# A state-space layer's depthwise convolution: from VectorE taps to diagonal matmuls, with one POOL/DVE split changed beside it

## The reference

```python
x, z = jnp.split(u @ in_w.T, 2, axis=-1)
xpad = jnp.pad(x, ((0, 0), (D_CONV - 1, 0), (0, 0)))
xc = conv_b + sum((xpad[:, k:k + L, :] * conv_w[:, k] for k in range(D_CONV)))   # D_CONV = 4
x = jax.nn.silu(xc)
xdbl = x @ xp_w.T                                  # 16 for dt, 16 for B, 16 for C
dt = jax.nn.softplus(xdbl[..., :DT_RANK] @ dt_w.T + dt_b)
dA, dBx = jnp.exp(dt[..., None] * A), (dt * x)[..., None] * Bm[:, :, None, :]
h = a * h + bx;  y = einsum('bdn,bn->bd', h, c)    # a scan over the 56 positions
y = (ys + x * Dp) * jax.nn.silu(z);  return y @ out_w.T
```

## Time and profile before

| What | us |
|---|---|
| median of three runs | 6076.04 (6052.26 to 6079.0) |
| the profiled execution | 6076.68 |
| its span, first to last instruction | 6074.9 |
| busy: DVE / POOL | 5261.9 / 5284.9 |
| busy: PE / ACT | 4575.6 / 3463.7 |
| mean granted TensorE clock | 0.871 of full speed |
| `prepare` and `attention` | until about 315 |
| `mambas`, first half: first scan at | 370.8 |
| `mambas`, second half: first scan at | 3109.2 |
| `finish` begins | 5798.6 |

### The profile page before, as it was taken

One profiled execution on the slowest core, in us unless ns is written; L12 is line 12 of the kernel. 1 busy time (PEld: TensorE's weight loads), 2 busy tenths in 40 slices (PEclk: granted clock), 3 DMA queues, 4 the chain that ended last, 5 costly groups with the idle time before them and its releaser, 6 DMA issues. The chain is left out here.

```text
span 6074.9 us, 66572 instructions
## 1 busy us (share of the span) xinstructions
PE 4575.6 (75%) x23774; PEld 3368.0 (55%) x23774; DVE 5261.9 (87%) x4001; ACT 3463.7 (57%) x5270; POOL 5284.9 (87%) x2694
## 2 busy tenths in 40 slices
PE   6957777777777777777667877777777777777689
PEld 5835555555555555555535555555555555555544
DVE  3469999999999999999969999999999999999900
ACT  0046666666666666666546666666666666666511
POOL 0059999999999999999959999999999999999900
PEclk8978888888888888888878888888888888888899
DMA  4123323232231322323123223232231323323164
GB/s 152 69 105 95 107 62 107 62 103 90 79 107 62 104 83 84 109 62 104 59 78 98 86 83 107 62 104 78 88 108 61 107 68 98 98 71 104 55 210 142
DMA packets 220096, 563.52 MB, mean 93 GB/s; under 512 B 27794, under 2 KB 94226, under 8 KB 218228
## 3 DMA queue, kind: packets, MB, share of 16 engines
q1 hardware_dynamic: 203956, 532.52, 28.0%
q10 hardware_dynamic: 15808, 26.75, 1.2%
HBM read 499.06 MB, written 60.13 MB: 92 GB/s over the span
## 5 line engine op out<-in xcount | busy, mean ns | idle before, releaser
L879 POOL TENSOR_TENSOR dbx<-dtx,b_all 128x896 f32<-128x896 f32 x1792 | 3701.3, 2091 | 0.2
L701 ACT ACTIVATE mamba_ps<-dt,w 128x448 f32<-128x448 f32 x3584 | 2136.4, 629 | 1660.5 <-DVE hc L828 1213.9
L654 PE MATMUL mamba_ps<-ident,hc 128*112 128x128 f32 x14336 | 2096.9, 300 | 968.2 <-POOL hc L886 944.1
L654 PEld LDWEIGHTS mamba_ps<-ident,hc 128*112 128x112 f32 x14336 | 1804.1, 147 | 1413.6 <-POOL hc L886 1053.6
L821 DVE TENSOR_TENSOR_SCAN mamba_ps<-mamba_ps,dbx 128x896 f32<-128x896 f32 x1120 | 2252.1, 2011 | 67.1 <-POOL dbx L879 61.7
L821 DVE TENSOR_TENSOR_SCAN hc<-mamba_ps,dbx 128x896 f32<-128x896 f32 x672 | 1353.1, 2013 | 141.3 <-ACT mamba_ps L701 141.3
L886 POOL TENSOR_TENSOR hc<-hc,c_all 128x896 f32<-128x896 f32 x672 | 1402.6, 2087 | 67.6 <-DVE hc L821 64.8
L828 DVE TENSOR_TENSOR hc<-mamba_ps,c_all 128x896 f32<-128x896 f32 x1120 | 1214.7, 1085 | 78.5 <-DVE mamba_ps L821 2.4
L582 PE MATMUL mamba_ps<-u,w 128*128 128x448 f32 x1792 | 881.4, 622 | 198.4 <-DVE x L801 142.8
L582 PEld LDWEIGHTS mamba_ps<-u,w 128*128 128x128 f32 x1792 | 365.2, 226 | 454.8 <-issue 224.8
L619 PE MATMUL mamba_ps<-w,sz 128*112 128x256 f32 x1792 | 491.2, 435 | 72.1 <-DVE sz L810 72.1
(11 more groups left out here) (98 smaller groups left out, 2597.5 us busy)
## 6 DMA issues: line engine op xcount, KB each, us to landing
b_all<-bc_scratch SPq DMA_DIRECT2D x448, 448.0 KB, 6.4
c_all<-bc_scratch SPq DMA_DIRECT2D x448, 448.0 KB, 6.1
u<-u_scratch SPq DMA_DIRECT2D x56, 448.0 KB, 8.8
y_scratch<-ytok SPq DMA_DIRECT2D x56, 448.0 KB, 3.2
src<-y_scratch SPq DMA_DIRECT2D x56, 448.0 KB, 4.6
xb<-in_x SPq DMA_DIRECT2D x4, 3136.0 KB, 12.0
u_scratch<-ub ACTq DMA_DIRECT2D x28, 448.0 KB, 8.2
src<-in_x SPq DMA_DIRECT2D x28, 448.0 KB, 6.8
```

Source lines behind the costliest of these rows:

```text
L654: ins = nc.tensor.matmul(y_ps[j % 2][:, c * 128:(c + 1) * 128], hc[g][:, e * T + c * TCH:e * T + (c + 1) * TCH], ident[:, :], start=False, ...
L701: ins = nc.scalar.activation(decay[g % 2][:, e * T:(e + 1) * T], blk(dt[t % 2], j), ACT.Exp, scale=w[:, c:c + 1])
L879: nc.gpsimd.tensor_tensor(view(dbx[g % BX_RING], 0, [[T, 2], [1, T]]), view(dtx[t % 2], j * T, [[0, 2], [1, T]]), view(b_all, 2 * g * T, [ ...
```

## The change

The convolution is made by PE. DVE makes, at the start of a half, 16 diagonal matrices of the convolution's weights (`taps`), beside the four of `skip`. ACT takes x_j as a plain copy. Four new items a tile, c0 to c3, are each four matmuls, a diagonal matrix by x_j shifted by 0 to 3 positions within each sequence, summed in a work bank; ACT takes c_j with the bias into x_j's place. `silu_x` follows c3. The DVE taps go. SCHEDULE has the new items, and y3 is made, taken and gated earlier. To make room in SBUF for `taps` the ring of dbx has 6 buffers and not 8. And POOL weighs 10 of 32 slots where it weighed 12.

```diff
 SCHEDULE = {
-    "x0": (0, 2), "x1": (2, 3), "x2": (5, 6), "x3": (7, 8), "y3": (10, None), "out0": (13, 14), "out1": (15, 16),
-    "y0": (16, None), "xp": (18, 19), "dt0": (19, 20), "dt1": (20, 21), "dt2": (21, 22), "dt3": (22, 23), "y1": (23, None),
-    "z0": (24, 25), "z1": (26, 27), "z2": (27, 28), "z3": (28, 29), "y2": (30, None),
+    "x0": (0, 1), "x1": (1, 2), "c0": (3, 5), "c1": (4, 6), "y3": (6, None), "x2": (7, 8), "x3": (9, 10), "c2": (10, 11),
+    "c3": (12, 13), "out0": (13, 14), "out1": (15, 16), "y0": (16, None), "xp": (18, 19), "dt0": (19, 20), "dt1": (20, 21),
+    "dt2": (21, 22), "dt3": (22, 23), "y1": (23, None), "z0": (24, 25), "z1": (26, 27), "z2": (27, 28), "z3": (28, 29),
+    "y2": (30, None),
 }
-FRONT = ("x0", "x1", "x2", "x3", "xp", "dt0", "dt1", "dt2", "dt3", "z0", "z1", "z2", "z3")
+FRONT = ("x0", "x1", "c0", "c1", "x2", "x3", "c2", "c3", "xp", "dt0", "dt1", "dt2", "dt3", "z0", "z1", "z2", "z3")
-MID, END = 0, 1
-TAP_AT = {
-    (2, MID): (0, 1), (2, END): (0, 2), (3, MID): (0, 3), (3, END): (1, 1), (5, MID): (1, 2), (5, END): (1, 3),
-    (7, MID): (2, 1), (7, END): (2, 2), (8, MID): (2, 3), (8, END): (3, 1), (10, MID): (3, 2), (10, END): (3, 3),
-}
-TAKE_Y_AT = {4: 3, 12: 0, 20: 1, 28: 2}
-GATE_AT = {11: 3, 16: 0, 24: 1, 31: 2}
+TAKE_Y_AT = {3: 3, 12: 0, 20: 1, 28: 2}
+GATE_AT = {7: 3, 16: 0, 24: 1, 31: 2}
-BX_RING, HC_RING = 8, 8
+BX_RING, HC_RING = 6, 8
 def by_pool(n):
-    return n % GP in (1, 4, 6)
+    return n % (2 * GP) in (1, 4, 6, 10, 14)
...
-        skip = sb("skip", DB * 128)
+        skip, taps = sb("skip", DB * 128), sb("taps", DB * DCONV * 128)
...
+                def conv(t, j):
+                    raw = Item(t, f"x{j}")
+                    pe.wait_ge(work_free[raw.slot], raw.freed())
+                    b = take(Item(t, f"c{j}"))
+                    for back in range(DCONV):
+                        k = (j * DCONV + DCONV - 1 - back) * 128
+                        ins = nc.tensor.matmul(seqs(b[:, 0:T])[:, :, back:SEQ], taps[:, k:k + 128],
+                                               seqs(blk(x[t % 2], j))[:, :, 0:SEQ - back], start=(back == 0), stop=(back == DCONV - 1))
+                    ins.then_inc(work_ready, 1)
...
-                        pe.wait_ge(skip_ready, t // TILES * DB + DB)
+                        pe.wait_ge(diag_ready, t // TILES + 1)
...
+                        nc.scalar.copy(blk(x[t % 2], j), take(it)[:, 0:T]).then_inc(work_free[it.slot], 1)
+                    elif name[0] == "c":
                         nc.scalar.activation(blk(x[t % 2], j), take(it)[:, 0:T], ACT.Identity,
-                                             scale=w[:, W_CW + j * DCONV + DCONV - 1:W_CW + (j + 1) * DCONV],
-                                             bias=w[:, W_CB + j:W_CB + j + 1]).then_inc(acc_ready, 1)
+                                             bias=w[:, W_CB + j:W_CB + j + 1]).then_inc(work_free[it.slot], 1)
...
-                nc.vector.tensor_tensor_scan(dst, h, dbx[g % BX_RING][:, :], 0.0, ALU.mult, ALU.add).then_inc(scan_done, 1)
+                nc.vector.tensor_tensor_scan(dst, h, dbx[n % BX_RING][:, :], 0.0, ALU.mult, ALU.add).then_inc(scan_done, 1)
...
+                        for k in range(DB * DCONV):
+                            ins = nc.vector.tensor_scalar_mul(taps[:, k * 128:(k + 1) * 128], ident[:, :], w[:, W_CW + k:W_CW + k + 1])
+                        ins.then_inc(diag_ready, 1)
-                        for j, back in TAP_AT.values():
-                            conv_tap(t, j, back)
```

More of the change, by code:

```diff
@@ L474, in mambas @@
         work_ready, work_free = sem("work_ready"), [sem(f"work_free{p}") for p in range(2)]
-        acc_ready, conv_chain = sem("acc_ready"), sem("conv_chain")
         silu_ready = sem("silu_ready")
@@ L481, in mambas @@
         scan_done, hc_ready, pc_ready, sums_done = sem("scan_done"), sem("hc_ready"), sem("pc_ready"), sem("sums_done")
-        skip_ready, ytr_ready = sem("skip_ready"), sem("ytr_ready")
+        diag_ready, ytr_ready = sem("diag_ready"), sem("ytr_ready")
         ones_set, restart_set = sem("ones_set"), sem("restart_set")
@@ L607, in front_item @@
                         in_proj(t, name, int(name[1]) * 128)
+                    elif name[0] == "c":
+                        conv(t, int(name[1]))
                     elif name[0] == "z":
@@ L723, in silu_x @@
                 def silu_x(t):
-                    it = Item(t, "x3")
+                    it = Item(t, "c3")
                     act.wait_ge(work_free[it.slot], it.freed())
@@ L790, in _ @@
             def _(dve):
[L791 to L805, removed]
                 def gate(t, j):
@@ L834, in _ @@
                         for j in range(DB):
-                            nc.vector.tensor_scalar_mul(skip[:, j * 128:(j + 1) * 128], ident[:, :], w[:, W_D + j:W_D + j + 1]).then_inc(skip_ready, 1)
-                        for j, back in TAP_AT.values():
-                            conv_tap(t, j, back)
+                            nc.vector.tensor_scalar_mul(skip[:, j * 128:(j + 1) * 128], ident[:, :], w[:, W_D + j:W_D + j + 1])
+                        for k in range(DB * DCONV):
+                            ins = nc.vector.tensor_scalar_mul(taps[:, k * 128:(k + 1) * 128], ident[:, :], w[:, W_CW + k:W_CW + k + 1])
+                        ins.then_inc(diag_ready, 1)
                     for n in range(SLOTS):
@@ L847, in _ @@
                                 gate(t - 1, j)
-                        if not last(t) and (n, MID) in TAP_AT:
-                            conv_tap(t + 1, *TAP_AT[n, MID])
                         if not by_pool(n):
                             weigh(SLOTS * t + n)
-                        if not last(t) and (n, END) in TAP_AT:
-                            conv_tap(t + 1, *TAP_AT[n, END])
                     if last(t):
@@ L878, in make_dbx @@
                     upto(pool, scan_done, n + 1 - BX_RING)
-                    nc.gpsimd.tensor_tensor(view(dbx[g % BX_RING], 0, [[T, 2], [1, T]]), view(dtx[t % 2], j * T, [[0, 2], [1, T]]),
+                    nc.gpsimd.tensor_tensor(view(dbx[n % BX_RING], 0, [[T, 2], [1, T]]), view(dtx[t % 2], j * T, [[0, 2], [1, T]]),
                                             view(b_all, 2 * g * T, [[T, 2], [1, T]]), ALU.mult).then_inc(dbx_ready, 1)
```

## The result

The changed kernel takes 6039.4 us (median of 20 runs, 6021.4 to 6058.9) against 6075.6 for the one before (20 runs), a ratio of 0.9949, 95% interval 0.9937 to 0.9961. It is faster by half a percent, where 2.3% were forecast; the time lies inside the range of 5865 to 6050, near its upper end. The profiled execution took 6041.8 us, its span 6040.0.

The account below looks back on a forecast made before the run. DVE with ACT's lateness was taken as the bound, POOL 1.2 us a tile behind. Saving 3.2 us in 54 periods (-173) plus 30 for fronts gave -143 from 6076.7: 5934 us, own range 5895 to 5975, stated range 5865 to 6050.

Parts of the forecast that it names:

- a tile without PE's clock: Each of 54 periods: 95.6 - 3.1 (DVE) + 1.1 (silu_z) - 1.2 (out1) = 92.4 us.
- new stall behind silu_z: Slot 3: ACT's chain takes 7.4 us, DVE without taps only 6.3, so a new stall of +1.1 a tile.
- stall behind silu_x: Slots 16 and 17: the scan was 2.23 us late; a shorter wait for out1 takes 1.2 off.
- PE's part of a tile: Convolutions on PE: 32 matmuls, 12.8 to 19.6 us a tile, costed at nothing within a tile.
- fronts: Serial stretch before each half's first scan: 28 us for 13.4, +15 a half, +30 in all (+25 to +38).
- DVE's sum: DVE's tile before: scans, weighs, taps and bare weighs 90.7 us, plus 2.6 waiting and 2.3 for gates, 95.6.
- POOL's floor: POOL's tile after the change: 44 passes, 89.8 + 0.4 = 90.2 us, below the 92.4 forecast.
- signs of being wrong: DVE waits for POOL in each tile, ACT waits for a convolution or dt, or the period is above 94.
- The 0.4 that is left of 2.6 (softplus) stays: Of DVE's 2.6 us a tile waiting for ACT, 0.4, put down to softplus, was to stay unchanged.
- The rival that said so: PE's lower clock delays dt blocks in each tile: period 96.4, 6152 us; decides above 36 of 54 periods; chance 0.11.
- the second rival: PE late in slots 10 to 15, out1's wait grows by some 0.7: 94.3 a tile, 6037 us; chance 0.19.
- out1's bound: ACT's wait for out1 at slot 16: change between 0 and -1.4, taken as -1.2; range effect 65 us up, 11 down.

Follow-up runs that it names:

- two kernels: Changed kernel with out1 taken at slot 17, y3 at slot 4 and POOL weighing 12 of 32 slots, 6020.5 us; kernel before with out1 at slot 17, 6003.1 us.
- The run that fills it: Changed kernel plus three extra matmuls, their result overwritten, on PE between x_proj's sums and dt0: 5915.1 us, ratio 0.9742.
- one number: Kernel before, taps still on DVE, with ACT taking out1 at slot 17, behind silu_x: 6003.1 us, ratio 0.9896.
- 5912: Changed kernel with z0 made by PE right behind xp at slot 18, not 24, and taken by ACT at slot 19: 5912.1 us, ratio 0.9730.
- both entries moved: Changed kernel with ACT taking out1 at slot 17, behind silu_x, and y3's sums at slot 4, behind silu_z: 5868.4 us, ratio 0.9663.
- out1 alone: Changed kernel with only ACT's take of out1 moved to slot 17, behind silu_x: 5903.4 us, ratio 0.9731.

## Why the prediction was wrong, point by point

| Step | Forecast | Measured |
|---|---|---|
| a tile without PE's clock | 92.4 us | 92.63 |
| new stall behind silu_z | +1.1 | 0.98 |
| stall behind silu_x | 1.03 | 1.32 |
| PE's part of a tile | 12.8 to 19.6, costs nothing | 12.6 busy; costs nothing by its length |
| stalls at the dt items | 0.4, as before | 0.2 in 18 periods, 2.0 to 4.0 in 36 |
| mean period | 92.4 | 94.27 and 94.75 |
| POOL | 90.2, not binding | not binding; as a bound 94.2 at 12 slots |
| fronts | +30 (25 to 38) | +7.1 and at most +13.8 |
| last tiles | 0 | +2.3 each |

**Right:** what bound the kernel, DVE's sum to two tenths of a microsecond (with 0.3 too little at slot 17 made up by 0.1 and 0.2 too much at slots 4 and 25), the stall behind silu_z, POOL's floor (two kernels sit on it, at 94.2 and 94.3), PE having room for the convolutions. The period of the undisturbed tile stands in the profile as forecast. Two of the signs of being wrong that the prediction named came about: ACT waits for dt, and the mean period is above 94.

**Wrong** is the sentence "The 0.4 that is left of 2.6 (softplus) stays". It held what the dt items cost to be unchanged, since none of their instructions were, and gave all of it to softplus; behind four dt items at the higher level it is 0.19, and the other 0.2 was the clock's already. Each of 36 periods loses 2 to 4 us there, 101 us over all: 54 x 92.63 would be 165 us less than before, and 63.5 came. The rival that said so was there, with its price (4.0 a tile; the long periods are 2.0 to 3.9 above 92.63, but for one of 5.9 at the start) and its turning point (36 periods), and it had 0.11, for two reasons that did not carry. "It is rare before" was read from one period of 99.57: rare, 4 of 54, was only that the clock stayed low through all dt items; it was low at dt0 in 46, and in 44 it came back in time, tile after tile, at the same period. Nothing said that another period would do so. And "the convolutions fill idle stretches of PE" was true of slots 0 to 13, whereas the stretch that counts, at slot 18, was left as it was. The run that fills it is what shows that it is this stretch.

That the time lies inside the stated range is not to the mechanism's credit: the range reached to 6050 for the sake of the second rival, and the forecast's own, 5895 to 5975, misses. That one was also too narrow for what it is said to hold, since 65 us from out1's bound alone lead from 5934 to 5999.

The stall at slot 17 was mis-sized by 0.3: PE brings out1 0.53 us late and not 0.2. The fronts were over-priced: the four convolutions took 12.0 us at the higher clock level, where 15 were put, and in the first front x_proj and the dt items ran at the higher level too, where they had not before.

```profile
326.31 3.21 DVE L829 TENSOR_SCALAR taps<-ident,w 128x128 f32<-128x128 f32 x16
...
329.63 5.83 PE L577 MATMUL mamba_ps<-u,w 128*128 128x448 f32 x8 [25.22 <-DVE taps L829]
...
335.30 6.02 PE L586 MATMUL mamba_ps<-x,taps 128*128 128x448 f32 x16
...
352.16 1.70 ACT L734 ACTIVATE x<-x 128x1792 f32<-128x1792 f32 x1
...
377.94 2.03 DVE L813 TENSOR_TENSOR_SCAN mamba_ps<-mamba_ps,dbx 128x896 f32<-128x896 f32 x1 [48.42 <-POOL dbx L868]
```

From PE's first matmul to SiLU it is 352.16 - 329.63 = 22.5 us, where it was 13.4: +9.1, and the 16 diagonals +3.2. But x_proj then took 3.21 us and not the 4.90 of the earlier trace rows, and the dt items 3.40 and not 5.34, so the first scan came only 7.1 later. This is luck and not a saving of the change: PE had been idle for 3.73 us ahead of x_proj, as in the second front, in which they took 4.90 and 5.00, and the way to the first scan became 13.8 longer.

Two parts of the change were not run by themselves: the ring of 6 dbx buffers and the earlier y3. The ring can have cost little, since DVE waited for dbx six times in all, 100.7 us, of which 99 are the two starts.

## What to carry to other kernels

A sum along the engine that binds gives the undisturbed period well, but an engine with room to spare can still set the time by its clock: look for a stretch in which TensorE is idle just ahead of items that another engine takes one by one, and put work that is needed there, no longer than the stretch. Ahead of a block that holds an engine for microseconds, leave nothing that could stand behind it. And before moving work between engines, look for one late hand-over in the schedule: here one number gave more than the move (6003 us against 6039), and the move gave its share (5903 against 6003) only once that was put right.

## What the runs showed of the hardware that was not expected

TensorE's clock fell behind an idle stretch of 2.6 us in one tile and not in the next, with the same instructions around it; the rows ahead of the two are alike, and no run here shows what decides. Once it had fallen it stayed at the lower level for 13.3 us with PE busy for all of them (in the kernel before, from 809.8 to 830.2, for 20.4 us with PE busy for 20.0), on transposes, x times D, matmuls of 17 rows and, at the end of the latter, the first of z; no run here separates these by kind. In an ordinary tile of the kernel before it came back within dt1, on the same instructions. With both entries moved, PE is idle for about 3.5 us ahead of x_proj, and x_proj met the lower level in 38 of 54 periods; with out1 alone it is 4.0 us and 48.
The Trainium skill ("TensorE: Matmul & The Clock Gate", A second HAM failure mode) tells of a kernel in which TensorE idles briefly between groups of matmuls and the clock goes up and down, with the median matmul still at its fast duration and only the throughput lower. The trace agrees that short idleness ahead of a group is enough; but here the single dt items are nearly twice as long (1.86 for 1.01 us) while it lasts, and that is what costs.

Three versions end within 12 us of each other by quite different means (5903, 5912, 5915). What they have in common is a shorter idle stretch ahead of dt0: 0.14, 1.11 and 0.31 us for 2.57. What stays open is what decides, with the same stretch, whether the clock falls and how long it then stays low.
